# A four-layer graph network: lanes ordered by an estimated clock, clears and table steps put elsewhere

## The reference

```python
h = relu(layernorm(x)); x = x + L0(h)   # three attention layers side by side, 4 heads of 64, summed
h = relu(layernorm(x)); x = x + L1(h)   # attention + a Mamba scan over nodes ordered by degree + noise, then merge
h = relu(layernorm(x)); x = x + L2(h)   # weighted neighbour sum, two 256x256 products, leaky relu, row norm
h = relu(layernorm(x)); x = x + L3(h)   # neighbour sum of h @ M, plus h @ W, relu
# L0, for each l: s = leaky_relu(a1[dst] + a2[src]); alpha = softmax of s over each dst
#   out += act_l(segment_sum(alpha * ft[src], dst) + h_l @ res_W[l])     act = relu, tanh, elu
# L1 merge: h_local = LN(elu(agg / denom + x + b)); h_attn = LN(x + y[inv]);
#   gate = sigmoid(h_local @ wl.T + h_attn @ wg.T); h = gate*h_local + (1-gate)*h_attn
#   out = LN(h + relu(h @ ff1.T + b1) @ ff2.T + b2)
```

## Time and profile before

| | |
|---|---|
| median of three runs | 7553.96 us (7552.7 to 7565.87) |
| the profiled execution's own time | 7538.81 us |
| its span in the profile | 7537.0 us |
| busy, PE / DVE / ACT / POOL | 70% / 71% / 44% / 57% |
| mean granted clock of PE | 0.866 of full speed |

### The profile page before, as it was taken

The page is one execution under the profiler, slowest core; times in us unless marked ns, Lnnn a source line. Parts: engine busy times, 40 slices in busy tenths (PEclk is TensorE's granted clock), DMA queues, the critical chain, the costliest instruction groups (busy, mean ns, idle before and its releaser), DMA issues. The chain is left out here.

```text
span 7537.0 us, 93661 instructions
## 1 busy us (share of the span) xinstructions
PE 5291.3 (70%) x19936; PEld 3387.9 (45%) x19936; DVE 5347.6 (71%) x11558; ACT 3290.1 (44%) x11052; POOL 4329.7 (57%) x4197
## 2 busy tenths in 40 slices
PE   4656878888888834647777776687666665666665
PEld 4623444444444423224444443465444444444544
DVE  7667678888888864358999997576666665555554
ACT  1123556666666622669899897454000000000000
POOL 2150066655666436027777777433777775777776
PEclk9978989999999965779999998798787887788787
DMA  6113288888888855248999998523666666666666
GB/s 202 19 63 108 109 287 281 277 281 273 279 275 279 244 201 188 92 163 311 321 326 325 322 323 253 145 88 98 231 230 234 228 233 185 215 222 222 223 219 190
DMA packets 557348, 1651.02 MB, mean 219 GB/s; under 512 B 135727, under 2 KB 249019, under 8 KB 528106
## 3 DMA queue, kind: packets, MB, share of 16 engines
q0 software_dynamic: 230192, 816.00, 35.7%
q1 hardware_dynamic: 291372, 799.55, 29.4%
q10 hardware_dynamic: 35372, 30.97, 1.4%
HBM read 1171.96 MB, written 701.99 MB: 249 GB/s over the span
## 5 line engine op out<-in xcount | busy, mean ns | idle before, releaser
L1270 POOL DMA_INDIRECT rows_e<-hidden,unit_src x1760 | 1676.0, 952 | 589.5 <-issue 510.6
L625 POOL DMA_INDIRECT rows_e<-table,unit_src x928 | 1023.6, 1103 | 845.7 <-PE acc_e L830 460.1
L1007 POOL DMA_INDIRECT rows_e<-table,unit_src x928 | 1072.3, 1156 | 362.4 <-issue 270.5
L819 ACT ACTIVATE rows_e<-rows_e 128x64 f32<-128x64 f32 x4640 | 1118.9, 333 | 1.9
L1379 PE MATMUL acc_e<-rows_e,same 128*128 128x256 f32 x1760 | 622.4, 500 | 457.2 <-DMA rows_e<-hidden,unit_src 433.4
L1091 ACT ACTIVATE rows_e<-rows_e 128x64 f32<-128x64 f32 x3712 | 920.0, 333 | 3.8
L1379 PE MATMUL acc_e<-rows_e,links 128*128 128x256 f32 x1760 | 613.4, 494 | 397.9 <-DMA rows_e<-hidden,unit_src 362.6
L1298 DVE SCALAR_TENSOR_TENSOR sums_e<-sums_e,unit_keep,acc_e 128x256 f32<-128x256 f32 x1024 | 486.4, 475 | 536.2 <-PE acc_e L1379 535.0
L830 PE MATMUL acc_e<-rows_e,unit_w 128*128 128x512 f32 (+1 forms) x1856 | 705.8, 527 | 143.7 <-DVE rows_e L812 101.8
L1423 ACT ACTIVATE turned_f<-turn_f 128x512 f32<-128x512 f32 x98 | 58.5, 597 | 1660.4 <-PE turn_f L1395 1660.4
L1379 PEld LDWEIGHTS acc_e<-rows_e,same 128*128 128x128 f32 x1760 | 418.6, 253 | 621.4 <-DMA rows_e<-hidden,unit_src 488.4
(11 more groups left out here) (517 smaller groups left out, 9720.2 us busy)
## 6 DMA issues: line engine op xcount, KB each, us to landing
staged<-sums_e SPq DMA_DIRECT2D x220, 1024.0 KB, 4.6
bc<-bc_rows SPq DMA_DIRECT2D x228, 896.0 KB
summed<-sums_e SPq DMA_DIRECT2D x464, 390.0 KB
summed<-sums_e SPq DMA_DIRECT2D x464, 130.5 KB
rows_e<-table,unit_src POOLq DMA_INDIRECT x1856, 5.2
hots<-hot_e SPq DMA_DIRECT2D x116, 256.0 KB, 4.9
hots<-unit_w SPq DMA_DIRECT2D x116, 256.0 KB, 4.9
rows_e<-hidden,unit_src POOLq DMA_INDIRECT x1760, 3.2
```

The lines of the kernel that those rows point to most:

```text
L625: pool.indirect_dma_start(self.rows[:, v, e, :], None, table, bass.IndirectOffsetOnAxis(unit_src[:, u, e:e + 1], 0)).then_inc(self.landed[ ...
L819: last = act.activation(r, r, ACT.Copy, scale=self.rows[:, v, e, self.WIDTH + h:self.WIDTH + h + 1])
L1007: pool.indirect_dma_start(self.rows[:, v, e, :], None, self.tab, bass.IndirectOffsetOnAxis(unit_src[:, u, e:e + 1], 0)).then_inc(self.land ...
L1270: pool.indirect_dma_start(self.rows[:, v, :], None, hidden[p], bass.IndirectOffsetOnAxis(index[:, u:u + 1], 0)).then_inc(self.landed[v // ...
```

## The change

It has seven parts.

1. The 19 clears of `own_firsts`, issued from ACT ahead of the first barrier, are issued from POOL inside the first pass, ahead of the clears of `summed`.
2. Five small vectors of layer one are loaded on ACT's queue with the first weights instead of at the start of the merge.
3. The table pass takes, after an item, two steps of `beside` at five items of nine and one at the other four.
4. The closing of layer zero is run by `by_clock` instead of `in_lanes`: each emitted step advances an estimate of when its lane is ready again and when its engine is free, and the lane that is ready first emits next.
5. The merge is run by `by_clock` too, with its steps beside.
6. At the end of the scan the remaining steps of the edge pass (`flush`) stand ahead of the last eight output products, the last gate's load is issued ahead of four waits, and the four last pieces of output go to buffers of their own.
7. A cleared tile is reused as the zero operand of one small product, and a memset goes.

```diff
+    def took(self, eng, n, after=0.15):
+        nc = self.nc
+        each = {id(nc.tensor): 0.2, id(nc.vector): 0.45, id(nc.scalar): 0.6, id(nc.gpsimd): 1.0}.get(id(eng), 0.5)
+        self.did.append((id(eng), each * n, after + (0.2 if eng is nc.tensor else 0.0)))
...
+        self.took(e, len(dmas), 2.0 + 1.5 * len(dmas))
...
+def by_clock(lanes, stage, gap, beside=iter(()), side=None, pace=1.3, blocks=range(0, T, 2)):
+
+    jobs = [(b, min(2, T - b)) for b in blocks]
+    running, ready, free = [None] * len(lanes), [gap * k for k in range(len(lanes))], {}
+    now, more = 0.0, True
+
+    def passed(begin, did):
+        for eng, busy, after in did:
+            start = max(begin, free.get(eng, 0.0))
+            free[eng] = start + busy
+            begin = start + busy + after
+        return begin
+
+    while jobs or any(running):
+        k = min((k for k in range(len(lanes)) if running[k] or jobs), key=lambda k: ready[k])
+        if more and now <= ready[k]:
+            if side:
+                side.did = []
+            more = next(beside, more) is not more
+            now = passed(now, side.did) if side and side.did else now + pace
+            continue
+        if running[k] is None:
+            running[k] = stage(lanes[k], k, *jobs.pop(0))
+        lanes[k].did = []
+        if next(running[k], k) == k:
+            running[k] = None
+        ready[k] = passed(ready[k], lanes[k].did)
...
-            chain.wait(act)
-            for first in own_firsts:
-                wide = first.rearrange("(p r) h -> p (r h)", p=P)
-                for c0 in range(0, wide.shape[1], AW):
-                    c1 = min(c0 + AW, wide.shape[1])
-                    act.dma_start(wide[:, c0:c1], zeros[:, 0:c1 - c0]).then_inc(cleared, 16)
-                    clears += 1
             settle()
...
             def clear_sums():
+                for first in own_firsts:
+                    wide = first.rearrange("(p r) h -> p (r h)", p=P)
+                    for c0 in range(0, wide.shape[1], AW):
+                        c1 = min(c0 + AW, wide.shape[1])
+                        yield pool.dma_start(wide[:, c0:c1], zeros[:, 0:c1 - c0]).then_inc(cleared, 16)
...
-                for _ in range(2):
+                for _ in range(2 if n % 9 in (0, 2, 4, 6, 8) else 1):
                     next(beside, None)
...
-                in_lanes(lanes, close_and_project, 4)
+                by_clock(lanes, close_and_project, 8.0)
...
+            sp.wait_ge(s_gated, 4 * NG + 2)
+            sp.dma_start(z_s[:, :], gate_rows[:, 1, NP:NP + TS]).then_inc(s_z, 16)
             for b in range(AHEAD):
                 sp.wait_ge(s_bc[b], 16 * (NG * K // AHEAD + 1))
...
-            pe.wait_ge(s_gated, 4 * NG + 4)
             for w in range(2):
                 gate(NG, 2 * NG, w, 1)
+            edges.flush()
+            pe.wait_ge(s_gated, 4 * NG + 4)
...
-            in_lanes(lanes, merge, 8, beside_merge(), 1)
+            by_clock(lanes, merge, 8.0, beside_merge(), chain)
```

More of the change, by code:

```diff
@@ L99, in step @@
         self.landing = False
+        self.took(eng, len(instructions))
     def apart(self, *pairs):
@@ L107, in apart @@
                     f().then_inc(self.sem, 1)
+            self.took(eng, sum(e is eng for e, _ in pairs))
         self.local += len(pairs)
@@ L137, in scatter @@
         self.landing = True
+        self.took(pool, len(instructions), 2.0)
     def gathers(self, pool, instructions, sem, value):
@@ L179, in in_lanes @@
         turn += 1
+    for _ in beside:
+        pass
+def by_clock(lanes, stage, gap, beside=iter(()), side=None, pace=1.3, blocks=range(0, T, 2)):
[22 more added lines that the diff above has]
+        ready[k] = passed(ready[k], lanes[k].did)
     for _ in beside:
@@ L316, in graph_stack_kernel @@
             chain.dma(sp, *copies)
-            clears = 0
-            chain.wait(act)
-            for first in own_firsts:
-                wide = first.rearrange("(p r) h -> p (r h)", p=P)
-                for c0 in range(0, wide.shape[1], AW):
-                    c1 = min(c0 + AW, wide.shape[1])
-                    act.dma_start(wide[:, c0:c1], zeros[:, 0:c1 - c0]).then_inc(cleared, 16)
-                    clears += 1
             settle()
+        clears = sum(-(-OWN // P * n // AW) for n in (L * H, H))
         class NodeCount:
@@ L408, in rank_nodes @@
                 tri_low = lsb("tri_low", [P, P])
-                one, zero = lsb("one", [P, 1], BF16), lsb("zero", [P, P], BF16)
+                one = lsb("one", [P, 1], BF16)
                 parts = lsb("parts", [P, T, 6])
@@ L414, in rank_nodes @@
                 sp.dma_start(keys[:, :], key_row.partition_broadcast(P)).then_inc(key_in, 16)
-                chain.apart((dve, lambda: dve.memset(one[:, :], 1.0)), (dve, lambda: dve.memset(zero[:, :], 0.0)),
+                chain.apart((dve, lambda: dve.memset(one[:, :], 1.0)),
                             (dve, lambda: dve.memset(parts[:, :, :], 0.0)),
                             (dve, lambda: dve.tensor_scalar(tri_low[:, :], iota[:, :], lane[:, 0:1], None, ALU.is_lt)))
-                chain.step(pe, lambda: pe.matmul(later_ps, zero[:, :], zero[:, 0:T], start=True, stop=False, skip_group_check=True))
+                chain.step(pe, lambda: pe.matmul(later_ps, zeros[:, 0:P], zeros[:, 0:T], start=True, stop=False, skip_group_check=True))
                 chain.wait(dve)
@@ L1177, in begin, with flush @@
                         slot(0, v, "first")
+            def flush(self):
+                for v in range(self.STORE):
+                    for slot in (self.act_slot, self.dve_slot, self.pe_slot, self.sp_slot):
+                        slot(self.ROUNDS, v, "last")
             def end(self, top):
                 n = self.ROUNDS
-                for v in range(self.STORE):
-                    for slot in (self.act_slot, self.dve_slot, self.pe_slot, self.sp_slot):
-                        slot(n, v, "last")
                 dve.wait_ge(self.s_neg, n * self.GROUPS)
@@ L1520, in run @@
                 nc.all_engine_barrier()
+        sides = ("ln_local_g", "ln_local_b", "ln_global_g", "ln_global_b", "ff1_b")
+        side_vecs = {n: sb(f"v_{n}", [P, a[f"L1_gnn_{n}"].shape[0] // P]) for n in sides}
         scored0 = ExitStack()
@@ L1553, in graph_stack_kernel @@
             weights += 1
+        for v, given in ((side_vecs[n], a[f"L1_gnn_{n}"]) for n in sides):
+            act.dma_start(v[:, :], given.rearrange("(c p) -> p c", p=P), allow_slow_non_contiguous=True).then_inc(weights_in, 16)
+            weights += 1
         load_noise(noise)
@@ L2524, in graph_stack_kernel @@
         names = ("gat_b", "ln2_g", "ln2_b", "ff2_b")
[L2525 to L2526 removed]
+        vecs = dict(side_vecs)
         weights_here = sem("weights_here")
@@ L2537, in graph_stack_kernel @@
             act.dma_start(v[:, :, :], a[f"L1_gnn_{n}"].rearrange("(c p) n -> p c n", p=P)).then_inc(weights_here, 16)
[L2538 to L2541 removed]
+        fb = vecs["ff1_b"]
+        all_loaded = 16 * (len(names) + 4)
         with ExitStack() as local:
```

27 lines of the change are left out of this document (12 added, 15 removed).

## The result

The changed kernel takes 7585.2 us (median of ten runs) where the kernel before takes 7553.3 us (ten runs, same chip): the ratio is 1.0044, 95% interval 1.0030 to 1.0057. It is slower by some 32 us; 133 us faster were forecast.

| stage | before, us | after, us | difference | forecast |
|---|---|---|---|---|
| to the first store of `summed` | 981.5 | 921.5 | -60 | -55 |
| edge pass, layer zero | 1680.1 | 1686.1 | +6 | 0 |
| closing of layer zero | 369.7 | 367.4 | -2 | -48 |
| from the closing to the scan | 370.3 | 376.4 | +6 | 0 |
| scan and its tail | 1390.6 | 1379.7 | -11 | -3 |

A forecast was written before the change was run, and what follows sets the result against it. Stages between barriers bound the kernel: POOL's blocked queue sets the closing's pitch, PE nearly bounds the merge. Terms 17 + 5 + 38 + 48 + 22 + 3 = 133 us off the median 7553.96 gave 7421, range 7365 to 7490.

The forecast's parts named there:

- Clears to POOL: Kernel start: without 19 clears on ACT the first barrier opens about 17 us earlier; POOL's added 10 us is covered.
- the open 6 us: Kernel start: the noise load's slow 6.02 us issue, perhaps due to the clears' traffic; not counted in the 17 us gain.
- Vectors loaded early: Merge's start: with five loads moved away, the first job starts 4 to 7 us earlier; 5 taken.
- Fewer steps beside: Table pass: 53 us of PE-only items go, costing 5 in the ranking and 10 in the planning; gain 38.
- Closing by clock: Layer zero's closing: POOL's waits for landed stores mostly covered, 2.5 of 12.8 us a job saved; gain 48 us.
- the low end of +10: Lower bound, in us, set on the gain of the closing by clock; the upper was about 89.
- Merge by clock: Layer one's merge: a third of PE's 65 us idle time is recovered; gain 22 us.
- 1.6 us x 25 = 40: Merge: largest loss thought possible, a job's idle time each, if PE's queue gets steps whose input is late.
- Scan's tail: End of the scan: gates start 3 to 4 us earlier with the load issued ahead; gain 3 us, bounds 0 and 10.
- (d): Rival, closing and merge: late-input steps in POOL's queue block seven lanes, 1.6 us a job more; time 7570, chance 0.05.
- (b): Rival, closing and merge: the clock's order is no better than turns, waits change names; sum 63, time 7491, chance 0.13.

The follow-up runs named there:

- e12: Changed kernel with the merge on turns and two steps beside in every turn of the table pass; ratio 0.9968 to the kernel before.
- e11: Kernel before with only the merge by clock, PE booked at 0.2 us; merge 549.7 us, ratio 1.0117.
- e8: Changed kernel with merge on turns, closing by clock, its turn on PE not waiting for the scatter's landing; closing 328.8 us, ratio 0.9862.
- e10: Changed kernel with merge and closing on turns, the closing's turn on PE not waiting for the scatter's landing; closing 367.0 us, ratio 0.9911.
- e5: Changed kernel with a PE instruction booked at 0.5 us instead of 0.2 in the merge's estimate; merge 458.8 us, ratio 0.9901.
- e2: Changed kernel with the merge's lanes starting 16 us apart in the estimate instead of 8; merge 547.1 us, ratio 1.0025.
- e9: Changed kernel with merge on turns, closing's clock booking landings and score scatters, turn on PE not waiting for the scatter; closing 340.3 us, ratio 0.9857.
- e15: Changed kernel, merge on turns, closing by clock, PE's turn not waiting for the scatter, nor three POOL lanes' scatter for their store; ratio 0.9848.

## Why the prediction was wrong, step by step

**Clears to POOL, 17 us: right at its place, 10 of it alone.** DVE goes on at 17.22 instead of 34.02, 16.8 us earlier, and POOL's 19 issues are not noticed. With the table's steps as before only 10 us of it reach the first store (e12 against e11). The traces tell where the rest goes: at the first product of the table e12 is 15.9 us ahead (348.2 against 364.1), at the load of `keys` 13.7, at the last compare 11.3, at the first store 9.8. The noise's load took 4.41 us instead of 6.02, so part of the open 6 us may have been the clears' traffic. What was saved is the time of issue, as the prediction had it: nineteen DMAs took 16.8 us ahead of a barrier, and their going was worth 10 at the first store. The Trainium skill (DMA: Bandwidth & Descriptors, Issuing engines are not separate DMA queues) says that starting DMAs from several engines saves only the issue time, and that this is usually small beside the DMA itself. The trace agrees with the first half; with nineteen of them, 16.8 us was not small.

**Vectors loaded early, 5 us: 1 us.** The weights ahead of it, which the prediction named as next, are what is late: DVE waits 13.37 us for `f`.

**Fewer steps beside, 38 us: 51.** All 53 us of the stretch came back. The two costs were both wrong, and came to 2 us together instead of 15. The sixteen items in the planning, put at 10 us, cost nothing: against e12 the changed kernel loads `keys` 11 us earlier (613.3 and 624.5). The fifteen in the ranking, put at 5 us at its end, cost 13: from `keys` to the last compare it takes 253.5 us against 240.9 (e12), the most of it in the one wait at its start, 12.98 us where it was 4.30. Together with the clears the start is 60 us shorter, forecast 55.

**Closing by clock, 48 us: some 5 (2, 5 and 13 in three pairs).** The step that failed is "The average wait was 53.2/13 = 4.1 us, so most are covered. I let 2.5 of the 12.8 us a job go". The wait was covered: 53.2 us in 13 times became 22.4 in 5, in 220 us of each. But the pitch did not follow (every third of POOL's loads comes 80 to 96 us after, 88 on the mean, where it was 90; forecast 72), since in the place of the covered wait stand PE's wait for a landed scatter (68.0 to 87.3 us in 200) and two other waits of POOL. The mechanism, POOL's wait for its landed store sets the pitch, was right for the order of turns: taken away by itself on three lanes it gives 32 us. What the prediction put at nothing is PE's queue, where the turn waits for a landed scatter; with that wait gone the same order is worth 38 us (e8 against e10). Of the bounds, the low end of +10 was too high for two of the three pairs.

**Merge by clock, 22 us: -90.** This is the step that decides the result. What failed is the path: a gain from PE's idle time, with a loss bounded at "1.6 us x 25 = 40", and of the booking only "books a PE instruction at 0.2 us, which is right only at the high clock", which the sum took no price from. At the high clock four records of 256 columns, that is two instructions, take 1.03 us, 0.5 us each. Booked at 0.2, a job's 36 PE instructions are 7 us in an estimate in which a round of seven jobs lasts 131 to 155, some 20 a job: PE is a third full there, and nothing makes the lanes share it. In truth it is the bound, 13.9 us of 17.9 a job. e5 changes this one number and gets all of the loss back, which shows the cause; e11, with the order alone put into the kernel before, loses as much. How much of the 90 is bunching and how much are dependent steps without filling between them stays open: e2 traded one for the other at the same price.

**Scan's tail, 3 us: 11 by the profiles**, 9 of them between the gates and the barrier. No run tested it apart, and the whole scan spreads by 20 us over the runs (1381.5 to 1402.5 on like chips), so it isn't shown to more than that.

**The rivals.** The result lies beyond (d), which had a loss of 1.6 us a job in both loops, by POOL's queue. It came in one loop, 3.6 us a job, by PE's. (b) named the booking of PE and took it for a reason to gain nothing.

**The best version.** The parts that don't touch the order, turns in the merge, and the closing by clock with the turn free of the scatter's landing: e8, e9 and e15 stand at 0.9862, 0.9857 and 0.9848, within each other's intervals, so which of the three is best is not shown; e15 is 1.5% faster than the kernel before and 2.0% faster than the changed one.

## What to carry to other kernels

An order made from an estimate is only as good as what it books for the engine that is the bound: check that the estimate's busiest engine and its pitch are those of the trace before trusting any order it gives. An order doesn't remove a wait, it puts somebody else's step in front of it; before forecasting a gain, ask of every engine's queue which waits stand in it, and look first whether the wait is needed at all: in the closing the new order was worth some 5 us with a needless wait left in and 38 without it. Where one engine is nearly full, as PE in the merge, an even round of turns is hard to beat, since each engine's queue then repeats the same filling pattern job after job.

## What the runs showed of the hardware

In the merge a hole of 12 to 14 us on PE is followed by matmuls at half speed (granted clock 0.61 over the window, 1.91 us for four records against 1.03); behind the idle of 6.12 us just ahead of the first such hole three records took 0.90 us, which elsewhere in the merge take 0.49. PE's busy time for the same 1625 instructions rises from 346.8 to 361.3 us; with a gap of 16 the clock was between 0.67 and 0.95 in most windows and PE's busy time 386.8 on that chip, against 350.2 with turns. So PE's busy share looks better than the work done in it, and an idle stretch is dearer than its length.
